# Layer 1's scatter of rows to the experts' slots waits for the first product of the first pass's second unit

## The reference

```python
xn = _rms_norm(x, norm_w)
xf = xn.reshape(-1, D)
logits = xf @ router_w.T
probs = jax.nn.softmax(logits, axis=-1)
_, top_idx = jax.lax.top_k(probs, TOP_K)
...
g = jnp.einsum('td,efd->tef', xf, gate_w)
u = jnp.einsum('td,efd->tef', xf, up_w)
h = jax.nn.silu(g) * u
h = h * comb_w[:, :, None]
y = jnp.einsum('tef,edf->td', h, down_w)
return y.reshape(B, S, D) + residual
```

## Time and profile before

| | |
|---|---|
| median of the runs | 1564.41 us (1563.14 to 1569.56) |
| span of the profiled execution | 1555.4 us |
| TensorE busy | 1457.8 us, 94% |
| VectorE busy | 1255.0 us, 81% |
| ScalarE busy | 880.7 us, 57% |
| GpSimd busy | 320.0 us, 21% |
| moved by DMA | 297.68 MB, 191 GB/s over the span |

### The profile page before, as it was taken

How to read it: one execution, slowest core, us unless ns; L and a number is a source line. 1 busy time by engine, 2 the same in 40 slices (tenths; PEclk the granted TensorE clock), 3 DMA queues, 4 the chain that set the end, 5 groups by cost and what they waited for, 6 DMA issues and landing times.

```text
span 1555.4 us, 38010 instructions
## 1 busy us (share of the span) xinstructions
PE 1457.8 (94%) x15152; PEld 1281.3 (82%) x15152; DVE 1255.0 (81%) x2182; ACT 880.7 (57%) x1275; POOL 320.0 (21%) x251
## 2 busy tenths in 40 slices
PE   7999899969999999999999899858999999999996
PEld 6777688866678999999997644448899999999995
DVE  8999777765666788888888789877978887888795
ACT  4114387765435677777773245545666666666651
POOL 1000156640300000000004067743600000000050
PEclk9999999988999999999999789869999999999999
DMA  7550000014756788988873011029888888888884
GB/s 192 151 135 24 11 1 2 2 59 146 211 180 225 270 290 308 291 304 298 306 285 109 18 34 33 18 106 339 281 291 304 285 301 283 307 286 302 290 270 108
DMA packets 55560, 297.68 MB, mean 191 GB/s; under 512 B 14063, under 2 KB 14319, under 8 KB 32433
## 3 DMA queue, kind: packets, MB, share of 16 engines
q1 hardware_dynamic: 41761, 263.23, 49.6%
q0 software_dynamic: 13712, 33.26, 7.9%
HBM read 264.07 MB, written 32.34 MB: 191 GB/s over the span
## 4 chain that ended last, share of the span: by engine, by line
PE 74%; DVE 17%; ACT 3%; issue 2%; POOL 2%; DMA 1%; DVEq 0%; POOLq 0%; ACTq 0%; SPq 0%
PE ps L779 14%; PE ps L758 10%; PE ps L760 10%; PE ps L762 10%; PE ps L2405 5%; PE ps L2388 5%; DVE wl L1464 3%; PE ps L2325 3%; PE ps L2517 3%; DVE wl L1465 3%; PE ps L2311 2%; PE ps L2200 2%; POOL wl L1027 2%; PE ps L791 2%; DVE wl L635 1%
## 5 line engine op out<-in xcount | busy, mean ns | idle before, releaser
L758 PE MATMUL ps<-big,wh 128*128 128x176 f16 x2160 | 496.1, 240 | 8.6 <-DVE wl L635 6.4
L762 PE MATMUL ps<-big,wl 128*128 128x176 f16 x2160 | 496.2, 238 | 0.0
L760 PE MATMUL ps<-big,wh 128*128 128x176 f16 x2160 | 496.1, 238 | 0.0
L779 PE MATMUL ps<-big,wh 128*128 128x176 f16 x2160 | 262.7, 238 | 1.0 <-DVE big L669 1.0
L779 PE MATMUL ps<-big,wl 128*128 128x176 f16 x1080 | 248.9, 239 | 0.0
L635 DVE SCALAR_TENSOR_TENSOR wl<-ext,wh 128x2304 f16<-128x2304 f32 x90 | 229.6, 2552 | 2.0 <-issue 1.8
L635 DVE SCALAR_TENSOR_TENSOR wl<-raw,wh 128x2304 f16<-128x2304 f32 x90 | 229.5, 2550 | 0.0
L554 ACT ACTIVATE wh<-raw 128x2304 f16<-128x2304 f32 x90 | 190.4, 2117 | 55.9 <-PE ps L779 55.4
L758 PEld LDWEIGHTS ps<-big,wh 128*128 128x128 f16 x2160 | 208.6, 97 | 12.5 <-DVE wl L635 6.0
L554 ACT ACTIVATE wh<-ext 128x2304 f16<-128x2304 f32 x90 | 190.5, 2117 | 47.9 <-PE ps L779 33.7
L760 PEld LDWEIGHTS ps<-big,wh 128*128 128x128 f16 x2160 | 211.2, 98 | 0.2
(11 more groups left out here) (373 smaller groups left out, 2811.5 us busy)
## 6 DMA issues: line engine op xcount, KB each, us to landing
raw<-in_units SPq DMA_DIRECT2D x54, 1152.0 KB
ext<-in_units SPq DMA_DIRECT2D x54, 1152.0 KB, 5.6
raw<-in_units SPq DMA_DIRECT2D x36, 1153.0 KB, 5.8
ext<-in_units SPq DMA_DIRECT2D x36, 1153.0 KB, 5.8
raw<-in_units_s SPq DMA_DIRECT2D x16, 769.0 KB, 4.3
ext<-in_units_s SPq DMA_DIRECT2D x16, 769.0 KB, 4.6
x_slots<-logs SPq DMA_DIRECT2D x1, 8976.0 KB
big<-x_slots POOLq DMA_DIRECT2D x17, 528.0 KB, 8.4
```

Of the source, the lines that this page charges most:

```text
L758: nc.tensor.matmul(o, wh[:, u % RING, w_], x_, start=c == 0 and m == 0, stop=False, skip_group_check=True)
L760: nc.tensor.matmul(o, wh[:, u % RING, w_], xTl[:, c, 0:ph.n], start=False, stop=False, skip_group_check=True)
L762: ins = nc.tensor.matmul(o, wl[:, u % RING, w_], x_, start=False, stop=c == KC - 1, skip_group_check=True)
L779: ins = nc.tensor.matmul(o, l_[:, u % RING, w_], r_, start=first and k == 0 and c % 2 == 0, stop=last and k == 2, skip_group_check=True)
```

## The change

GpSimd waits, ahead of layer 1's scatter, until `ph_1.up` is 2, that is until TensorE has ended the up product of the second unit of the first pass. Nothing else is changed.

```diff
             for t in range(NT):
                 pool.wait_ge(s_split, t + 1)
                 nc.gpsimd.tensor_tensor(rowl[t], z[:, t, :], rowh[:, t, :], ALU.subtract).then_inc(s_rest, 1)
+            pool.wait_ge(ph_1.up, 2)
             scatter(1, z)
             pool.wait_ge(s_tab, 2)
             ffn_pool(pool, ph_1, last_pass(pool), rows_joined)
```

## The result

The changed kernel takes **1580.55 us** (median of four runs, 1576.3 to 1581.3) against 1563.78 us of the kernel before in the same comparison: a ratio of 1.0113, interval 1.0075 to 1.0151, that is +12 to +24 us with +18 in the middle; the two medians differ by 16.8 us. The profiled execution has a span of 1579.8 us and took 1581.3 us, so 1.5 us lie around a span. The two profiled executions differ by 24.4 us. Of this 4.45 us lie ahead of the change: the product that picks the first pass's rows starts at 1049.72 in the changed kernel and at 1045.27 before.

A forecast was written before the change was run, and what follows sets the result against it. TensorE, busy 94% of the span, was taken as the bound, with 1.2 us slack behind the scatter. Stall +13.0, clock +2.0 and -1.5 given back make +13.5 us on 1564.4: 1578.0 us, range 1568 to 1586.

The forecast's parts named there:

- rival C: Layer 1's scatter, starved by unit loads to 0.063 MB/us, lands later: X = 1104.7, +19.5 us, 1584; chance 0.12.
- the forecast's own 0.70: Chance given to the main case, in which GpSimd requests the second pass's rows between 1092 and 1103.
- X: Moment GpSimd issues rows_in(1), the second pass's row request, after the scatter lands: 1085.28 before, forecast 1099.5, bounds 1092.0 and 1102.5.
- The start: First scatter instruction on GpSimd goes at about 1060.0 instead of 1042.77, 17.2 us later.
- the step on the landing: Scatter's bytes: 0.55 MB by 1067.2, remaining 3.29 MB at 0.114 MB/us until 1096.1, then 3.4 us until release.
- the tail: Time between the scatter's last bytes and GpSimd's release: up to 7.4 us before, forecast 3.4, between 1.5 and 7.4.
- The fetch: The second pass's rows arrive 7.6 us after GpSimd's request, at 1107.1.
- The early gain: VectorE's line 667 runs 0.37 us shorter without the scatter beside it; TensorE reaches line 742 at about 1093.7.
- Rival D: Units 3 to 5 load earlier, removing TensorE's 2.77 us wait and slow clock: -4.3 us; no chance of its own.
- The clock: TensorE runs at half clock for 3 to 5 us after its stall: +2.0 us.
- What comes back: Some rows_joined work falls in TensorE's stall, returning 1.5 of 2.7 us lost behind VectorE (bounds 0 and 2.7).
- Rival B: GpSimd's issuing, not the link, limits the scatter; X = 1085.5, no stall, 1561 to 1564; chance 0.16.

The follow-up runs named there:

- the later turning: The changed kernel with TensorE's turning of the fetched rows (line 742) one unit later in layer 1, behind up(0,9) instead of up(0,8): 1576.38 us, ratio 1.0089.
- up 1: The changed kernel with GpSimd's wait one product earlier, the scatter waiting until ph_1.up is 1: 1571.23 us, ratio 1.0067 to the kernel before.

## Why the prediction was right, point by point

I forecast +13.5 us (1578.0, 1568 to 1586) and the runs say +16.8, interval +12 to +24. The path was the one described; two terms were mis-sized, in opposite directions, and a third did not count. That the time came within 3.3 us of the forecast is in part luck: the release, the term that carries the sum, lay outside its bounds, a shorter fetch took part of it back, and by the sign named for it (a request after 1104) this was the time of rival C, not that of the forecast's own 0.70 (X from 1092 to 1103).

- **The start.** Forecast 17.2 us later; measured 17.2 (from -2.5 to 14.7).
- **The release** was forecast 39.5 us behind the first instruction, with bounds of 32.0 and 42.5. It came 47.0 us behind, outside the bounds: +7.5 us. In the step on the landing three parts failed. I had 0.55 MB moved in the first 7.2 us, as on the quiet link; in fact the first packet started 6.9 us behind the first instruction. I costed the slower issuing at nothing, since TensorE didn't feel it in the gather; the scatter did, 25.5 us in place of 18.0. And the last 0.09 MB did not come faster when the loads stopped: the link fell to 32 GB/s, and they still took until 1109.7. The shared rate was 0.128 MB/us for 0.114, a little better. Rival C's X of 1104.7 is nearer to the measured one (1106.9 when counted as in the kernel before) than mine of 1099.5, but its reason, a scatter starved to 0.063 MB/us, is not what happened.
- **Data and tail apart.** The packets of q0 in the two traces split the 47.0 and the 42.5 us further. In the kernel before, the last packet with rows in it ends at 1077.8, 35.1 us behind the first instruction, and 7.5 us go by until the release, in which q0 has nothing but packets of 4 and 8 bytes beside the loads. This is its row for 1078 to 1085:

```profile
q0 software_dynamic: 41, 0.00, 0.3%
```

In the changed kernel the rows are over 45.3 us behind the first instruction, and the release follows 1.7 us later. So the rows took 10.3 us longer (36.1 us forecast), and the tail, forecast as 3.4 us, was 5.8 us shorter than before: the prediction had the tail of before right (7.4 us, though from its own 1077.5 it would be 7.8) and saw that it would shrink. The mis-sized term is the moving of the rows, by 9.2 us.
- **The fetch** took 5.65 us instead of 7.6, on an idle link: -2.0.
- **The early gain.** Forecast 0.4 us; TensorE reached line 742 2.9 us sooner: 1.4 of the 2.77 us ahead of `up(0,2)`, and the slow clock behind them. Rival D was right about its being real. VectorE's stand ahead of `low(0,2)`, in its register load, fell from 1.75 to 0.51 us. But the stall ends with the landing, so the gain only made the wait longer (21.4 us for 13.4 forecast), as the prediction said of it.
- **The restart** lies 18.5 us later than before (forecast 13.0): 21.6 for the release, less 2.0 for the fetch, less the slack of 1.2.
- **The clock**: 0.50 for 3.0 us, so 1.5 us lost; forecast 2.0. (The 0.56 that the prediction gives for the 3 us after 1064.08 is of the window from 1063 on, which begins within the wait; from 1064 to 1067 it is 0.53.)
- **What comes back**: 1.4 us of waiting left of 2.7, so 1.3 back; forecast 1.5.
- **The sum** from these: 18.5 + 1.5 - 1.3 = 18.7. Read at GpSimd's request for the fourth pass's rows (1159.60 before, 1182.27 after, less 4.45) it is 18.2. The remaining 1.7 us of the spans' difference lie behind the last pass.
- **Rival B** (an issue-bound landing, no loss) is excluded by the wait of 21.4 us, and even with the loads all but gone the release comes 34 us behind the start, not 25.
- **Around the span** I left 9.0 us, taking the profiled execution for a median one. It is 1.5 us; the profiled execution of before was simply a fast one (1556.9 us by that). The forecast, made as a difference on the median, didn't suffer.

## What to carry to other kernels

Ask of a transfer that is moved who waits for its end, and how much room there is between the two: here 1.2 us, so that a start 12 us later cost some 10 us and one 17 us later some 17, while all that it could win was 4.4 us. A transfer that is issued into a busy stretch pays three times, in the slower issuing, in its late first bytes and in the shared link, so its duration can't be taken over from the quiet stretch. And a gain ahead of a wait is worth nothing until the wait is gone; first make room behind (the later turning), then move.

## What the runs showed of the hardware that I had not expected

**Each scatter instruction runs on five of the sixteen DMA engines.** From 1106 to 1111 q0 moved 0.09 MB in 49 packets, at an 0.08 share of the DMA engines, and GpSimd was held by it. The last 13 packets with rows stand one behind the other in the trace, without gap or overlap, from 1106.83 to 1109.72: twelve of 6144 bytes, 0.23 us each, and one of 3072. That is 26.5 KB/us, the share of one engine (with the link full, all sixteen move 413 KB/us, 26 for each), and it is 25 rows, a fifth of an instruction's 125. The kernel before shows the same from its other end: from 1045 to 1047, in the first 2.4 us in which rows move, five packets of q0 run at a time, a sixth only for moments. Its whole scatter has 600 packets of 6144 bytes and 50 of 3072, which is ten instructions times five shares of 25 rows. (The trace does not name the engines; the five follow from these counts.) The rows of q0, first of the kernel before, 1045 to 1047, then of the changed one, 1106.83 to 1109.72 (5 of 16 engines would be 31%, 1 of 16 would be 6%):

```profile
q0 software_dynamic: 31, 0.15, 29.5%
...
q0 software_dynamic: 13, 0.07, 5.9%
```

So one instruction by itself moves no more than some 0.13 MB/us (an estimate, five times 26.5 KB/us), and in the changed kernel the last share to be served sets the landing, which the free link did not hasten. The Trainium skill (DMA: Bandwidth & Descriptors, section "Specifications") gives some 27 GiB/s for one engine, which is 29 KB/us; the 26.5 KB/us of this trace lie a little below.

**Scatter instructions wait for VectorE.** A scatter instruction takes GpSimd some 1.2 us when VectorE leaves it alone and 2.0 to 3.6 us beside the 2.55 us operations of line 635. In the thirteen profiles that have the scatter, 72 of its 125 instructions take 1.19 to 1.36 us, and each of the other 53 ends 1.06 to 1.11 us behind the end of such an operation of VectorE, with the loads beside it or without them. The first one of the changed kernel (1064.39 to 1067.83) had this beside it, which ends at 1066.72:

```profile
1064.16 2.56 DVE L635 SCALAR_TENSOR_TENSOR wl<-ext,wh 128x2304 f16<-128x2304 f32 x1 [0.51 <-issue]
```

**A register load on VectorE stood longer with the scatter at its old place**: 1.07 to 1.75 us in the four profiles that have it there (1.75 in the kernel before), 0.51 in the changed kernel, 0.53 with the scatter at up 1, already under way. Since the last of these has both scatter and loads beside it, neither is shown as the cause; it stays open.
